# First node stage of a graph-network kernel: the PSUM-to-SBUF copy of the source rows on VectorE instead of ScalarE

## The reference, cut to what matters

```python
h = jnp.maximum(_layernorm(x, axis=-1), 0.0)
msg_in = jnp.concatenate([x[src], x[dst], edge_attr], axis=-1)     # x here is h
h1 = jax.nn.relu(msg_in @ msg_W1 + msg_b1)
messages = h1 @ msg_W2 + msg_b2
aggregated = jax.ops.segment_sum(messages, dst, num_segments=x.shape[0])
# then the node update, a second layer norm, and an attention layer over the same edges
```

## Time and profile before

| | us |
|---|---|
| median of 3 runs (4052.76 to 4057.73) | 4053.22 |
| the profiled execution | 4052.3 |
| its span in the trace | 4050.5 |
| first gather of the first edge pass begins | 69.86 |

### The profile page before, as it was taken

How to read it: one execution, slowest core, us unless ns; L and a number is a source line. 1 busy time by engine, 2 the same in 40 slices (tenths; PEclk the granted TensorE clock), 3 DMA queues, 4 the chain that set the end, 5 groups by cost and what they waited for, 6 DMA issues and landing times. The chain is left out here.

```text
span 4050.5 us, 117915 instructions
## 1 busy us (share of the span) xinstructions
PE 3054.5 (75%) x30845; PEld 2211.2 (55%) x30845; DVE 2072.5 (51%) x7909; ACT 1780.8 (44%) x4395; POOL 2983.4 (74%) x3154
## 2 busy tenths in 40 slices
PE   4778878778887778788857777777777777777776
PEld 3667666666666666666634444444444444444444
DVE  5344444444444444444435555655565565556555
ACT  4333333333333333333335555555555555555555
POOL 4777777777777777777747777777777777777775
PEclk8777777877777777777768888888888888888887
DMA  6555555555555555555423333333333333333332
GB/s 163 144 145 139 145 142 143 144 141 140 143 146 137 146 141 145 138 146 137 121 65 86 85 86 85 85 85 86 85 85 85 86 86 85 85 85 86 85 85 58
DMA packets 397865, 455.98 MB, mean 113 GB/s; under 512 B 156453, under 2 KB 296963, under 8 KB 397791
## 3 DMA queue, kind: packets, MB, share of 16 engines
q1 hardware_dynamic: 297295, 249.90, 22.4%
q0 software_dynamic: 100096, 205.00, 20.4%
q10 hardware_dynamic: 400, 0.20, 0.0%
HBM read 434.70 MB, written 20.07 MB: 112 GB/s over the span
## 5 line engine op out<-in xcount | busy, mean ns | idle before, releaser
L730 POOL DMA_INDIRECT m_ring<-tab_a,m_idx x1564 | 1483.5, 949 | 516.5 <-issue 508.9
L730 POOL DMA_INDIRECT t_ring<-tab_l,t_idx x1564 | 1478.3, 945 | 517.1 <-issue 458.9
L1192 PE MATMUL bank<-w,m_attr_t 128*128 128x128 f32 x3128 | 733.5, 363 | 91.2 <-DVE m_hot L1276 91.0
L1909 PE MATMUL bank<-t_hot_t,t_win 96*128 96x128 bf16 x1564 | 329.3, 238 | 514.0 <-DMA t_ring<-tab_l,t_idx 506.2
L1192 PEld LDWEIGHTS bank<-w,m_attr_t 128*128 128x128 f32 x3128 | 629.6, 249 | 146.6 <-issue 107.2
L1241 ACT ACTIVATE m_hid<-m_pre 128x512 f32<-128x512 f32 x391 | 246.4, 630 | 999.9 <-DVE m_pre L1286 986.0
L1286 DVE TENSOR_TENSOR m_pre<-bank,m_ring 128x512 f32<-128x512 f32 x391 | 270.2, 691 | 784.2 <-DMA m_ring<-tab_a,m_idx 439.4
L1918 PE MATMUL bank<-t_zt,att_wn 128*128 128x512 f32 x782 | 545.4, 788 | 0.7 <-DVE t_zt L2018 0.7
L1960 ACT ACTIVATE t_z<-bank 128x512 f32<-128x512 f32 x391 | 233.5, 597 | 667.0 <-PE bank L1911 639.7
L1909 PEld LDWEIGHTS bank<-t_hot_t,t_win 96*128 96x128 bf16 x1564 | 166.3, 108 | 603.4 <-issue 581.2
L2062 DVE TENSOR_TENSOR t_old<-acc,t_shrink 128x64 f32<-128x64 f32 x391 | 88.3, 226 | 695.8 <-ACT t_shrink L1973 609.4
(11 more groups left out here) (206 smaller groups left out, 5253.6 us busy)
## 6 DMA issues: line engine op xcount, KB each, us to landing
m_ring<-in_edge_attr_dram SPq DMA_DIRECT2D x390, 256.0 KB
m_row<-dst_rows SPq DMA_DIRECT2D x391, 128.0 KB
t_row<-dst_rows SPq DMA_DIRECT2D x391, 128.0 KB
m_ring<-tab_a,m_idx POOLq DMA_INDIRECT x1564
t_ring<-tab_l,t_idx POOLq DMA_INDIRECT x1564
m_win<-tab_b SPq DMA_DIRECT2D x391, 24.0 KB
t_win<-tab_r SPq DMA_DIRECT2D x391, 24.0 KB
tab_r<-n_r SPq DMA_DIRECT2D x49, 96.0 KB
```

The lines of the kernel that those rows point to most:

```text
L730: pool.indirect_dma_start(out=r.got[u][0:rows, j, :], out_offset=None, in_=table, in_offset=bass.IndirectOffsetOnAxis(ap=r.idx[half][0:row ...
L1192: pe.matmul(p_hid[q % 2][:, e], lhsT=attr_t[q % 2][:, e], rhs=k.w1[:, 2, :], start=True, stop=False)
L1909: pe.matmul(p_z[q % 2][:, e], lhsT=r.win[q][:], rhs=hot_t[q % 2][0:3 * W, e], start=True, stop=False)
```

## The change

The copy of the product out of PSUM leaves ScalarE's step and goes to VectorE's step, as `tensor_copy` behind the reciprocal and the negative mean of the same step, and ahead of the extra work of steps 4, 5, 8, 9 and 11. It keeps its waits (`a_ap` and `s_ast`) and its semaphore `a_a`. ScalarE's loop becomes one step shorter. The offset of three chunks stays.

```diff
-        for n in range(NC + 3):
+        for n in range(NC + 2):
...
                 last.then_inc(s["a_xn"], 1)
-            if 0 <= n - 3 < NC:
-                c = n - 3
-                act.wait_ge(s["a_ap"], c + 1)
-                after(act, s_ast[c % 2], 16 * (c // 2))
-                act.activation(at[c % 2][:, 0:size(c), :].rearrange("p t d -> p (t d)"), p_ab[c % 2][:, wide(c)],
-                               ACT.Copy).then_inc(s["a_a"], 1)
...
                 dve.scalar_tensor_tensor(out=nm[:, tiles(c)], in0=mv[:, tiles(c), 0], scalar=-1.0, in1=rs[:, tiles(c)],
                                          op0=ALU.mult, op1=ALU.mult).then_inc(s["a_nm"], 1)
+            if 0 <= n - 3 < NC:
+                c = n - 3
+                dve.wait_ge(s["a_ap"], c + 1)
+                after(dve, s_ast[c % 2], 16 * (c // 2))
+                dve.tensor_copy(at[c % 2][:, 0:size(c), :].rearrange("p t d -> p (t d)"), p_ab[c % 2][:, wide(c)]
+                                ).then_inc(s["a_a"], 1)
             if n == 4:
                 for b in range(min(2, NBLK)):
                     take_rows(b)
```

## The result

| | before | changed |
|---|---|---|
| median of 9 runs each, us | 4052.76 (4051.90 to 4057.73) | 4063.54 (4061.98 to 4066.89) |
| ratio, 95% interval | | 1.0028 (1.0019 to 1.0036) |
| span of the profiled execution | 4050.5 | 4065.1 |
| first gather | 69.86 | 81.59 |
| span behind the first gather | 3980.6 | 3983.5 |

The kernel became 10.8 us slower. A second set of runs on one chip gave 4064.06 against 4053.62, ratio 1.0028 (1.0017 to 1.0038), and its profile a first gather at 79.79 and 3979.3 us behind it. So the first gather moves the end, and what lies behind it stays within the few us by which executions differ. The difference is 0.28% of the time, small but outside the interval.

What follows compares the result with a forecast made beforehand. The first gather's start was taken to set the end, the rest running at GpSimd's pace. Middle 3.2 plus tail 7.1 gave 10.3 us; 4052.3 plus 10.3 is 4062.6, plus 0.9 for the median 4063.5 us, range 4059 to 4066.5.

Steps and rivals of the forecast that it cites:

- What bounds the kernel: Gather passes run at GpSimd's pace once started, so a shift of the first gather moves the kernel's end by as much.
- Price of the copy: Each 512-element copy out of PSUM on VectorE: 0.69 us, and 0.61 us until the next instruction starts.
- The half price: Lower bound for VectorE's copy: 0.35 us, if a contiguous copy ran two elements at a time.
- Middle: Copies waiting in VectorE's queue hold up the statistics ScalarE needs; those of chunk 10 start 3.20 us late.
- the walk: Step-by-step forecast from the held copy of chunk 2 to the count chain: first gather 10.3 us later; chance 0.72.
- Tail: End of the stage: count chain stands behind the last copy, no longer beside the last chunks; 7.1 us of overlap lost.
- Sum: First gather later by 10.3 us: 3.2 from lateness in the middle, 7.1 from lost overlap at the end.
- Edits at nothing: ScalarE's shorter loop, TensorE's bank waits, SyncE's stores and GpSimd's casts beside the early copies: no time lost.
- The port question: Whether VectorE's PSUM copies are held by GpSimd's casts through shared ports: claimed not, and no loss if held.
- Rival (a): Only the lost overlap at the end costs: +7.1 us, 4060.3 us; decided by chunk 2's copy starting before about 31; chance 0.14.
- Rival (b): Not slower: ScalarE sets the step throughout and its freed 5.8 us arrive at the end; +1.3 us, 4054.5; chance 0.06.
- Rival (c): First store lands later (3.7 instead of 2.3) or loop waits cost 0.1 to 0.2 us more: up to +13 us, 4066; chance 0.08.

Runs made afterwards that it cites:

- the run with the tail taken away: Changed kernel with the copies of the last three chunks (10, 11, 12) back on ScalarE: 4058.05 against 4053.04 us, ratio 1.0012; first gather 74.19 us.
- reordered kernel with added transposes: Kernel before, VectorE's waits for TensorE moved to where data is ready, plus 96 identity transposes ahead of TensorE's first step: 4050.87 against 4053.62 us, ratio 0.9993.

## Why the prediction was right

- **What bounds the kernel.** Right. The span behind the first gather was 3979.3 to 3983.5 us in ten profiles on the ordinary chips, with first gathers from 64.97 to 81.59.
- **Price of the copy.** 0.69 us, and 0.60 to 0.61 to the next instruction (33.58 to 34.18); predicted 0.69 and 0.61. The half price was not met.
- **Middle.** The mechanism is right, its size was right only on average. The step from landing to statistics of chunk 6 was 1.83 against 1.85 in the walk. Statistics of chunk 10 were expected 3.20 us late and were 4.27 and 2.01 late in the two profiles. The terms that were mis-sized: the landing of the first store was taken as fixed at 33.75 (33.58 and 32.61 here, 32.6 to 34.6 over the runs that don't edit it; with 32.61 the walk gives 2.06, and 2.01 came), and the clock was taken as 1.00 in the middle, where a product of 1.91 instead of 1.06 us came in the one profile and not in the other. The two errors happened to lie on both sides of the forecast.
- **Tail.** 7.1 us predicted. From the base rows on, the count chain moved from 2.68 us behind them (52.51 to 55.19) to 66.92 - 56.79 = 10.13 and, in the second profile, 65.12 - 54.52 = 10.60: 7.5 and 7.9. The excess of 0.3 and 0.8 over 7.14 is mainly TensorE's lower clock: the product of chunk 10 took 1.86 and 1.92 us instead of 1.58, and in the second profile its transposes took 1.11 us, where the first had 0.66. The run with only the last three copies on VectorE isolates the term: 6.67 with that product at 1.06, which is 7.2 with one of 1.58.
- **Sum.** 10.3 us for the count chain; 11.73 and 9.93 measured, 10.8 and 10.4 in the medians. The forecast of 4063.5 hit the median of 4063.54 to 0.04 us, which is luck, given the errors of both signs above.
- **Edits at nothing.** The port question was decided as argued: the copies of chunks 0 and 1 ran at 26.04 and 28.62 beside GpSimd's casts (25.28 to 29.57) in 0.69 us each. What was held was the negative mean between them, on SBUF: 0.49 us at 28.02, and 0.90 at 28.03 in the second profile, instead of 0.16. It cost nothing, as the prediction had said of such a hold, since the copy of chunk 2 at 33.58 sets the path.
- **Rival (a)**, only the tail: refuted by the run with the tail taken away, still 4.33 us late. Its point of decision was misplaced: the copies one step later, with transposes added, show that the middle can be brought down to about 0.5 us without an earlier store, by not letting the copy stand ahead of what ScalarE needs.
- **Rival (b)**, ScalarE's relief arrives: refuted. ScalarE's busy time in the stretch from 24 to 54 us fell from 25.0 us to 18.5 and 21.0 in the two profiles, about by the nine copies of 0.58 us that had started there, and the stage took longer. The Trainium skill, Perfetto Trace Analysis, section Optimizing Scalar/DVE Operations, gives a saturated VectorE as a reason to move work to ScalarE. No run here shows that case: neither engine was saturated (17.2 and 25.0 of 30 us). What decided was the order of the queue.
- **Rival (c)**, worse than the walk, is not what the medians show. Single executions had a late first store (34.64), but by another way than (c) names: it was issued late, at 32.20, and landed after 2.44 us, not 3.7.

Open: why single issues of SyncE's take longer in one execution than in another, which puts the first store up to 2.0 us apart over these runs (1.0 in the same kernel), and why TensorE's clock falls in one execution and not in the other. Nor was a third staging buffer tried, which would take the wait away without moving the copy.

## What to carry to other kernels

An engine's queue is in order, so moving an instruction moves its waits: ask what stands behind it and who waits for that, before asking which engine is less busy. Then ask what ran beside the moved work: a serial chain that used to overlap the last pieces is worth the overlap that is lost (7 to 8 us here, against 2 to 4 in the middle). And where the walk shows an engine waiting at a place where its data could be ready, reordering that queue may gain what the move was meant to (5.2 us here).

## What the runs showed of the hardware

TensorE's clock in a short stage differs between executions of one program. Its two levels are 1.2 and 2.4 GHz; four transposes took 1.09 to 1.12 us at the lower and 0.66 at the upper, eight passes of a product 1.92 and 1.06. The lower was seen after idle times of 3.35 and 3.49 us, but also a little after one of 1.93 (the copies one step later, at 34.30). One of 2.17 left it up, and so did one of 1.93 in the run with only the last three copies on VectorE, at 34.44; and in two kernels that are the same up to there the product of chunk 1 took 1.06 us (before, at 27.27) and 1.90 us (only the last three copies on VectorE, at 27.43). In a stage in which every engine waits for TensorE once a step, that makes spread: from the statistics of chunk 6 to those of chunk 10 the changed kernel took 14.49 us in its first profile and 13.19 in its second. That the changed kernel's executions spread more than those of the kernel before isn't shown: they lay 4.9 and 5.0 us apart, those of the kernel before 5.8 us in 9 and 4.2 in each of two sets of 31.

The landing of the first store was steady, 2.42 to 2.46 us after its issue in eight profiles; its issue, behind 29 others of mostly 0.43 us in one queue, was not (30.18 to 32.20). Issued at 26.77 it took some 5.2 us.

VectorE's instruction on SBUF of 0.16 us took 0.49, 0.90 and 1.81 us beside casts of GpSimd's, while its copies out of PSUM beside them kept their 0.69.

Windows of the reordered kernel with added transposes, which dropped in the middle, for how the level reads in a table by stretch (stretch, us, PE, PEld, DVE, ACT, POOL, PEclk, DMA share, GB/s):

```profile
36.00:45.00 9.00, 7.86 (x46) 7.69 (x47) 4.61 (x23) 7.34 (x19) 0.00 (x0) 0.62 0.28 83
```

There 0.62 is mostly the lower level; the same stretch reads 0.62 in the first profile of the changed kernel and 1.00 in the second.
